# A graph network's scatter loop: border sums placed in PSUM by ScalarE, border joins and the src table moved into the first steps

## The reference

```python
msg = relu((x @ W_m1.T + b_m1)[src] + (x @ W_m2.T + b_m2)[dst] + (edge_attr @ W_me.T + b_me))
msg = relu(msg @ W_net.T + b_net)
agg = segment_max(msg, src, num_segments=6250)        # 0 where a node has no edge
x   = layernorm(x + x @ W_o1.T + b_o1 + agg @ W_o2.T + b_o2)
```

## Time and profile before

| what | value |
|---|---|
| median of 3 runs | 3780.2 us (3772.44 to 3789.65) |
| profiled execution, its time | 3754.61 us |
| profiled execution, its span | 3752.6 us |
| mean granted clock of PE | 0.804 of full speed |
| PE busy | 2743.1 us, 73% |
| DVE busy | 1925.6 us, 51% |
| POOL busy | 1692.6 us, 45% |
| ACT busy | 1120.7 us, 30% |
| first scatter issued | at 141.94 us |

### The profile page before, as it was taken

The page is one execution under the profiler, slowest core; times in us unless marked ns, Lnnn a source line. Parts: engine busy times, 40 slices in busy tenths (PEclk is TensorE's granted clock), DMA queues, the critical chain, the costliest instruction groups (busy, mean ns, idle before and its releaser), DMA issues. The chain is left out here.

```text
span 3752.6 us, 82895 instructions
## 1 busy us (share of the span) xinstructions
PE 2743.1 (73%) x22172; PEld 2390.7 (64%) x22173; DVE 1925.6 (51%) x8319; ACT 1120.7 (30%) x2463; POOL 1692.6 (45%) x1819
## 2 busy tenths in 40 slices
PE   7877777776888878886699756666666666676667
PEld 6766666666776667764466545665666666666667
DVE  6644544433555555555588733444444444444446
ACT  3222222222344444444466621111111111111114
POOL 1455544555545454443311135555455454545443
PEclk8677767777899999888799877777777777777778
DMA  6322223111333333356588311111111111111111
GB/s 190 79 72 71 71 70 87 37 40 33 84 97 96 93 92 97 92 153 159 142 201 200 85 41 38 36 36 37 34 36 36 35 38 35 36 34 37 34 33 35
DMA packets 575909, 276.48 MB, mean 74 GB/s; under 512 B 499504, under 2 KB 542826, under 8 KB 575546
## 3 DMA queue, kind: packets, MB, share of 16 engines
q1 hardware_dynamic: 225752, 107.85, 11.9%
q0 software_dynamic: 55104, 99.54, 9.7%
q10 hardware_dynamic: 294818, 66.10, 8.4%
HBM read 151.69 MB, written 127.59 MB: 74 GB/s over the span
## 5 line engine op out<-in xcount | busy, mean ns | idle before, releaser
L1298 POOL DMA_INDIRECT edge_in_src_order<-ring_u,ring_p x784 | 772.1, 985 | 782.1 <-issue 493.0
L1979 POOL DMA_INDIRECT a_rows<-src_table,idx x782 | 744.0, 951 | 744.4 <-DMA idx<-src_c 521.2
L2059 PE MATMUL ps_h<-a_rows,ident 128*128 x1664 | 325.8, 327 | 276.4 <-issue 275.7
L2059 PEld LDWEIGHTS ps_h<-a_rows,ident 128*128 128x128 f32 x1664 | 276.6, 235 | 311.3 <-issue 310.8
L2099 ACT ACTIVATE h<-ps_h 128x512 f32<-128x512 f32 x208 | 124.2, 597 | 1151.8 <-remote 812.3
L2028 DVE TENSOR_SCALAR ohd_f<-iota_b,dloc_c 128x128 f32<-128x128 bf16 x832 | 186.0, 292 | 509.9 <-remote 424.8
L2064 PE MATMUL ps_h<-bpart,dstT_b 128*128 x1664 | 317.2, 351 | 171.5 <-ACT dstT_b L2093 137.0
L2064 PEld LDWEIGHTS ps_h<-bpart,dstT_b 128*128 128x128 f32 x1664 | 278.1, 253 | 202.0 <-issue 201.8
L1395 DVE TENSOR_TENSOR_SCAN top<-same,top,bank 96x512 f32<-96x512 bf16 x221 | 281.6, 1274 | 174.5 <-remote 109.0
L1337 DVE TENSOR_TENSOR prior<-bank,earlier 128x512 f16<-128x512 f32 x196 | 134.8, 688 | 454.6 <-remote 369.1
L2016 DVE TENSOR_TENSOR hsumT<-hsumT,ps_s 128x128 f32 x832 | 239.3, 288 | 191.1 <-issue 83.5
(11 more groups left out here) (347 smaller groups left out, 5104.4 us busy)
## 6 DMA issues: line engine op xcount, KB each, us to landing
u_in<-edge_in_src_order SPq DMA_DIRECT2D x222, 192.0 KB
running_max<-row ACTq DMA_DIRECT2D x222, 192.0 KB
rowt<-src_row SPq DMA_DIRECT2D x222, 130.0 KB
running_max<-zero_rows ACTq DMA_DIRECT2D x37, 576.0 KB
key_b<-dst_of_edges ACTq DMA_DIRECT2D x832, 0.5 KB
edge_in_src_order<-ring_u,ring_p POOLq DMA_INDIRECT x784
a_rows<-src_table,idx POOLq DMA_INDIRECT x782
dge_attributes_by_column<-in_edge_attrT SPq DMA_DIRECT2D x8, 784.0 KB, 12.1
```

The costliest lines, as they stand in the source:

```text
L1298: pool.indirect_dma_start(u_d, bass.IndirectOffsetOnAxis(ring_p[:, j:j + 1], 0), ring_u[:, j, :], None).then_inc(sent[i % 4], 16)
L1979: pool.indirect_dma_start(a_rows[:, 4 * u + j, :], None, a_d, bass.IndirectOffsetOnAxis(idx[:, u % 4, j:j + 1], 0)).then_inc(got[u % 4], 16)
L2059: m.matmul(ps_h[k][:, j, :], ident[:], a_rows[:].rearrange("p c d -> p (c d)")[:, bass.ds(slot[j], D)], start=(j == 0), stop=False, skip_g ...
```

## The change

- `x1T` is no longer under the ring, so the ten DMAs that load it back on POOL's queue go.
- The src table leaves the setup block. It is made in the hooks of steps 7 to 36 (M1 = 7): at one step the products of five blocks, at the next two the two subtractions, each with its copy on ACT, all in bank 6.
- The border's one-hots, turns and copies move into the setup block, where quads 0 to 8 are made by POOL and 9 to 13 by DVE. The turned rows lie in `m1`'s memory. The border's products (PE) and joins (DVE) move to the hooks of steps 0, 1 and 2 (5, 5 and 4 quads).
- `product` loses its four matmuls with `ident`. A new stage of ACT, `seed`, copies the four border rows into bank 4 ahead of the four that are left.
- Of the 49 clearing DMAs for half 1, 20 instead of 16 are on SP's queue and 29 instead of 33 on POOL's.
- SP's `pipeline` for the src order has no cut at turn 111. SP waits for all groups to be sent at turn 90, when the scatter's steps are over, instead of at turn 111.
- The counts of half 2 start one step later, marks, ranks and tables too.

```diff
@@ product, tensor
-                            wait(pe, u_ready, i)
+                            pe.wait_ge(seeded, i + 2)
                             for j in range(4):
-                                m.matmul(ps_u[:, j, :], dstT[:, u, j, :], m2[:, bass.ds(at[j], F)],
-                                         start=(j == 0), stop=False, skip_group_check=True)
-                            of = offsets(nc, mybir.EngineType.PE, xs_row[:, 4 * i:4 * i + 4], ND * F - F)
-                            for j in range(4):
-                                mm = m.matmul(ps_u[:, j, :], ident[:], more[:, bass.ds(of[j], F)],
-                                              start=False, stop=True, skip_group_check=True)
+                                mm = m.matmul(ps_u[:, j, :], dstT[:, u, j, :], m2[:, bass.ds(at[j], F)],
+                                              start=False, stop=(j == 3), skip_group_check=True)
@@ scalar
+                        def seed(i, u, n):
+                            act.wait_ge(x_chain, ND)
+                            act.wait_ge(seeded, i + 1)
+                            wait(act, u_ready, i)
+                            at = offsets(nc, mybir.EngineType.Activation, xs_row[:, 4 * i:4 * i + 4], ND * F - F)
+                            for j in range(4):
+                                last = s.copy(ps_u[:, j, :], more[:, bass.ds(at[j], F)])
+                            last.then_inc(seeded, 1)
-                        order = [("d", 2, first), ("c", 1, turned), ("c", 3, rows), ("d", 5, rows_out_of), ("d", 6, store), ("d", 0, stage)]
+                        order = [("d", 2, first), ("c", 1, turned), ("c", 3, rows), ("c", 2, seed), ("d", 5, rows_out_of), ("d", 6, store), ("d", 0, stage)]
@@ hooks, tensor
+                            if M1 <= now < M1 + 3 * NT:
+                                b, k = divmod(now - M1, 3)
+                                src_table(b) if k == 0 else rest(b, k - 1)
+                            if now < len(XQ) - 1:
+                                for q in range(XQ[now], XQ[now + 1]):
+                                    border_product(q)
@@ hooks, vector
+                            if now < len(XQ) - 1:
+                                for q in range(XQ[now], XQ[now + 1]):
+                                    border_join(q)
@@ hooks, scalar
+                            if M1 <= now < M1 + 3 * NT:
+                                src_limb(*divmod(now - M1, 3))
@@ the waits behind the border part, in sync, scalar, tensor and vector
-                        sp.wait_ge(x_chain, ND)
-                        act.wait_ge(x_chain, ND)
-                        pe.wait_ge(x_chain, ND)
-                        dve.wait_ge(x_chain, ND)
@@ setup block, gpsimd and vector
+                            for q in range(BY):
+                                border_rows(pool, g, q, 0)
+                            for q in range(BY, BX):
+                                border_rows(dve, v, q, 0)
@@ sync
-                            if isinstance(i, int) and i in (0, GS):
-                                groups_sent(sp, CS if i == 0 else CG)
+                            if isinstance(i, int) and i == 0:
+                                groups_sent(sp, CS)
...
-                        pipeline(sp, GB, [(12, landed), (0, load_u)], done=C_STEPS - K0, cuts=(GS,), early=KS + 4)
+                        groups_sent(sp, CG)
+                        pipeline(sp, GB, [(12, landed), (0, load_u)], done=C_STEPS - K0, early=KS + 4)
@@ gpsimd
-                        for lo in range(0, NP, 5 * P):
-                            hi = min(lo + 5 * P, NP)
-                            g.dma_start(x1T[:, lo:hi], xT[:, lo:hi]).then_inc(x_back, 16)
```

More of the change, by code:

```diff
@@ new lines, in border_pick, with border_local @@
+                def border_pick(pe, m, r, of):
+                    pe.wait_ge(pick_set, r + 1)
+                    for k in range(CK):
+                        mm = m.matmul(of[:, 64:64 + ND], dst_c[:, k, :], pick[:, k, :], start=(k == 0), stop=(k == CK - 1))
+                    mm.then_inc(picked, 1)
+                def border_local(dve, v, r, of):
+                    dve.wait_ge(picked, r + 1)
+                    v.scalar_tensor_tensor(out=split_l[:], in0=iota_f[:, 0:ND], scalar=-float(BD), in1=of[:, 64:64 + ND],
+                                           op0=ALU.mult, op1=ALU.add).then_inc(border_set, 1)
+                    dve.wait_ge(border_set, 3 * r + 3)
@@ L1051, in _ @@
                                 chunks_act(act, nc.scalar, k0, bank[4:6], bank[6:8])
+                                for q in range(BX):
+                                    border_copy(act, nc.scalar, q, 1, bank[2:4])
                                 ranks_act(act, nc.scalar, c0, 0, bank[3])
@@ L1209, in gnn, with turn_of_half_1, in_turns @@
                 OUT = MARKS[1] + NB // 2 + 6
-                assert OUT + 4 < K0 and MARKS[0] + NB < RANKS < MARKS[1] - 2 and MARKS[1] + NB // 2 + 3 < K0 and PADS + 13 < CS
+                assert OUT + 4 < K0 and M1 + 3 * NT < RANKS - 1 and MARKS[0] + NB < RANKS < MARKS[1] - 2 and MARKS[1] + NB // 2 + 3 < K0 and PADS + 13 < CS
+                def turn_of_half_1(now):
+                    return max(0, now - K0)
+                def in_turns(order, now):
+                    ds = range(turn_of_half_1(now), turn_of_half_1(now + 1))
+                    for kind, lag, work in order:
+                        if kind == "c":
+                            step([(kind, lag, work)], "c", CG, now)
+                        elif ds:
+                            step([(kind, lag, work)], "d", GB, ds[0])
+                    for t in ds[1:]:
+                        for kind, lag, work in order:
+                            step([(kind, lag, work)], "d", GB, t)
                 def groups_sent(eng, count):
@@ L1506, in _ @@
                         for now in range(C_STEPS):
-                            for kind, lag, work in order:
-                                step([(kind, lag, work)], kind, CG if kind == "c" else GB, now - (0 if kind == "c" else K0))
+                            in_turns(order, now)
                             hooks(now)
@@ L1618, in border_turn, with border_product @@
[L1618 to L1623 removed]
+                        def border_product(q):
+                            wait(pe, x_chain, 4 * q - 3 if q > 1 else 0)
+                            for j, b in enumerate(border_blocks(q)):
+                                mm = m.matmul(bank[6 + q % 2][:, F * j:F * j + F], dstT_x[:, b - 1, :], m2[0:BD, F * b:F * b + F], start=True, stop=True)
+                            mm.then_inc(x_ready, 1)
```

319 lines of the change are left out of this document (156 added, 163 removed).

## The result

The changed kernel takes 3722.7 us (median of 4 runs, 3719.5 to 3725.0), the one before 3779.0 beside it (4 runs, 3772.4 to 3789.7): a ratio of 0.9853, with an interval of 0.9829 to 0.9877, so 56 us less. I had predicted 3616, in a range of 3530 to 3715. The direction is right; the size is off by two thirds, and the time lies outside the range.

What follows compares the result with a forecast made beforehand. PE was taken to bound the scatter loop, starved during POOL's long runs. Loop 153 + setup 6 + border 11 - SP's wait 6 = 164 us off 3754.6: 3591 profiled, 3616 against the median; range 3530 to 3715.

Steps and rivals of the forecast that it cites:

- The bound: Scatter loop: PE sets the pace, busy 0.75, 0.72 and 0.82 of its windows, and does less during POOL's long runs.
- The border rows by ACT: Scatter loop: line 1571's 250 us leave PE, 21 return for the src table; of 229 net, 153 us saved.
- Setup and border: Ahead of the loop: setup block saves 6 us (bounds -3 and 9), border part 11 (bounds 5 and 16).
- SP's wait: At turn 90, ahead of the src-order work: costs 6 us, bounds 0 and 20 if POOL is some groups behind.
- Rival 1: Scatter loop: all of PE's saving passes, 229 + 11 = 240 us, time 3540; chance 0.13.
- Rival 2: Scatter loop: POOL's pauses set the gain, 71 + 11 = 82 us, time 3698; chance 0.13.
- Rival 3: PE's granted clock falls and takes part of the gain back; chance 0.11, its size not in the text given.
- Rival 4: Scatter loop: ACT becomes the bound with `seed` at 3.9 us a step, 51 us slower, 3831; chance 0.09.
- Straight code: Scatter loop: straight code is its form, and PE's gaps in it come with POOL's runs; no size given.
- The range: Whole kernel: 3530, below all of PE's saving passing, to 3715, above POOL's pauses setting it; slower cases left out.
- gives all back: Scatter loop: a `seed` of about 3 us a step cancels the whole gain; chance 0.04.
- my own sign of being wrong: Scatter loop: steps hardly change though PE's busy time has fallen by 1.2 us each.

Runs made afterwards that it cites:

- long comparisons: Comparisons of kernels in which the kernel before the change took 3770 to 3772 us in the median (two of seven); the given pair, 3779 and 3723 us, counts as one.
- no_seed3: Changed kernel with TensorE's four identity products back in place of ScalarE's four border copies: 3773.6 us, 1.0009 of the kernel before.
- cut_third: Changed kernel with SyncE's wait for the last scatter put back from turn 90 to turn GS: 3721.5 us, 0.9867 of the kernel before.
- short comparison: Comparison of kernels in which the kernel before the change took 2660 to 2667 us in the median (five of seven).
- plain_cut: Changed kernel with ordinary DMAs to fixed places for the scatters by index (no src sorting) and SyncE's wait back at turn GS: 3140.7 us, 0.8331 of the kernel before.
- no_border: Changed kernel without any border rows in the sums, neither ScalarE's copies nor TensorE's identity products: 2669.2 us, 1.0032 of the kernel before.

## Why the prediction was wrong, step by step

- **The bound.** "PE is the bound, and where POOL has run long without a pause PE gets less done than it could": the second half decided. In the long comparisons the pace comes from PE together with the scatters' holds on it, in the short ones from GpSimd itself.
- **The border rows by ACT**, the failed step: "one for one is 229", of which I took two thirds, 153, "because PE's busy share is far over POOL's". Measured in the loop: 26, that is 46 to 47 for the copies less 21 for the rest of the change. Two things were wrong in it. The 250 us are the busy time of line 1571 alone, which partly overlaps that of line 1567: the two lines together were busy 485.7 us before and line 1604 alone 278.3 after, and the whole of PE lost 154 us, or 149 between `no_seed3` and `cut_third`. And of the 141 of these that lie in the loop, a third became time: 59 came back as more holds and other gaps of "issue", 36 as waits. A busy share says how full an engine is, not whether work taken off it frees time. The copy's price, 237 ns for my 240, was right.
- **Setup and border**: 6 + 11 = 17 predicted, 17.0 measured; 20.6 in the short comparison.
- **SP's wait**: 6 predicted, about 4 in the long case at the first gather (between two comparisons), nothing measurable at the end. In the short case 24, over the bound of 20 that I gave "if POOL is some groups behind"; there it is.
- **Rival 1** (all passes) fell. **Rival 2** (POOL's pauses, 71 us in the loop) had the right half of the mechanism, and its signs came, more "issue" on PE and POOL's longer runs, but its price did not: POOL's pauses between scatters, those over 0.45 us, fell by 37 us, from 565 to 527. It is the nearest in time, 3698. **Rival 3** is that PE's granted clock falls and takes a part of the gain back; its chance of 0.11 rested on an estimate of mine that no run shows. The clock did fall, from 0.76, 0.77 and 0.90 to 0.72, 0.67 and 0.85. With the scatters by index gone it was 0.96 (`plain_cut`, 125 to 600 us), so the low clock came with the holds; what it cost beside them is not separated. What a matmul of line 1571 takes at two clocks, the trace of the kernel before shows: 421 ns where 0.50 was granted (532 to 546 us) and 275 ns where 1.00 was (1090 to 1110 us), a factor of 1.53. **Rival 4** (ACT): a copy takes 237 ns, so its price is refuted, and in the given pair `product` waits only 18 us for the copies. Its mechanism is there where nothing holds PE, 104 us in `plain_cut`. `no_border`, which gains nothing without the copies, ran in a short comparison alone, where GpSimd's sum sets the pace.
- **Straight code**, the loop's form: the same straight code ran without holds in `plain_cut` (1.0 us of "issue" between 300 and 400 us, for 28.4 in the changed kernel), so straight code alone does not bring them; whether it has a part in them beside scatters by index is not shown.
- **The range** ended at 3715 because I gave "gives all back" 0.04. What happened is close to my own sign of being wrong, that the loop's steps hardly change though PE's busy time has fallen: 831.6 and 832.2 us for the first 110 groups, though PE's busy time there fell too.

## What to carry to other kernels

Before taking work off the busiest engine, ask what its idle time stands next to: if gaps of "issue" come with another engine's DMAs by index, try what the kernel does without those DMAs before anything else. Here leaving them out, and the sorting with them, was worth 16% of the kernel before (3180 us in one run, for 3771.7), where taking line 1571 off TensorE was worth 1.4%. When an edit moves a queue's wait to an earlier turn, cost it for the case that the queue waited for is many groups behind. The version to keep is the change with SyncE's wait left at turn GS: 0.992 and 0.993 of the kernel before in the short comparisons and 0.987 in the long one, where the change itself is 1.001 and 1.003, and 0.985 in the given pair. The two long ratios don't differ beyond their intervals.

## What the runs showed of the hardware

- TensorE's starts held to a grid of 0.72 us in stretches of up to 8 us. In the scatter loop this was seen only with four or more DMAs by index of 0.99 us in one go, and only in some comparisons: the same programs ran without it in others, there with POOL's scatters back to back, 0.3 us apart. One chip was in a comparison of either kind. What decides it stays open, and so does what in the chip sets the 0.72 us.
- The same kernel, the one before, took 3770 us with holds and 2663 without. With no DMAs by index in the loop the two kinds of comparison agree on the loop's end within 0.5 us (1047.05 and 1046.63); behind the first gather they stay 569 us apart (2015.4 and 1446.2), for reasons not looked into.
- One ordinary DMA of four blocks of 128 rows of 384 bytes took GpSimd 0.75 us (`plain_cut`), four by index 4 x 0.99 and three pauses of 0.3.
